# Moving the DRAM casts of the weights: one per four slots in steps 3 to 12, none in steps 13 to 16, the rest from the second chunk's second step on

## The chip, the cores and the metric

The kernel runs on the 8 cores of one Trainium2 chip. Each core has a matrix engine (TensorE, PE), a vector engine (VectorE, DVE), a scalar engine (ScalarE, ACT), a general engine (GpSimd, POOL) and a sequencer that only issues transfers (SyncE, SP). Sixteen DMA engines per core move the data for all of them. Every core computes two of the sixteen sequences and no core talks to another. The metric is the device time of the slowest core, in microseconds.

## The reference, cut

A state-space layer (Mamba) with a post-norm, then a feed-forward layer with a low-rank term and a second post-norm, on x of shape 16 x 2048 x 1024:

```
xc, z = split(x @ W_in.T)                     # 2 x 2048 columns
xc    = silu(conv4(xc) + conv_b)
xp    = xc @ W_x.T                            # B (16), C (16), dt (1)
delta = softplus(dt * w_dt + b_dt)
h_t   = exp(delta*A) * h_(t-1) + (delta*xc) B_t      # 16 states per channel
y     = (sum_n h_t C_t + D*xc) * silu(z)
x     = layernorm(x + y @ W_out.T)
h     = gelu(x @ W1.T + scale * (x @ m1.T) + b1)
x     = layernorm(x + h @ W2.T + scale * (h @ m2.T) + b2)
```

`m1` and `m2` are built from 16 tokens of the sequence (the low-rank term).

## The kernel before

**Tiling.** A core's 2 x 2048 tokens are cut into 8 chunks of 512 tokens (`NC = 8`, four chunks to a sequence, `CPS = 4`). The 2048 inner channels are 16 tiles of 128. One tile of one chunk is a *step*; steps are numbered through, 0 to 127, and chunk c has the steps 16c to 16c + 15. A step has 8 *slots* (`NP`), so a chunk has 128 slots (`CS`). In each slot DVE runs two recurrences (`tensor_tensor_scan`, L1014: one state of 128 channels over 512 tokens), in every second slot one product of four states with C (`hm`, L1024), and in the fifth slot of a step the gate of the step before (`yy`, L1035). PE feeds the recurrences (`ps_dbx`, L528) and sums the states (`ps_y`, L548), ACT makes the decays (`da`, L859).

**What shares the slots.** While chunk c runs its recurrences, the other matrix work is laid into the same slots by `plan()`: the input projection and convolution of chunk c + 1 (`X1`, `X2`, `Z`), and all that follows the recurrences of chunk c - 1 (`OUT`, `F1`, `F2` and the statistics `ST`). So chunk 0 (slots 0 to 127) carries no `OUT`, `F1` or `F2`, and chunk 1 (slots 128 to 255) is the first that does. Every engine goes through the slots in order; what an engine has to do in a slot stands in `pe_at`, `act_at`, `pool_at`. POOL is held to DVE's pace: in each even slot s it waits until the product s/2 is made.

**Where weights come from.** The weights lie in DRAM as float32 (`wts`, 122 tiles of 128 x 1024). The projections that run before slot 128 take theirs from a transfer issued by POOL that converts on the way (`WFIRST`, `wr<-wts`, L1076, 49 tiles). Every later use takes a bfloat16 copy, `w_scr`, in DRAM. This copy is made once, by *casts*: DRAM-to-DRAM transfers issued by POOL (`w_cast`, L1081, `w_scr<-wts`), 31 of them, each of four tiles (1 MB written) but one of two. The input gets a bfloat16 copy too, one cast per chunk (`XCAST`, `x_cast`, L1062, `xt_scr<-xt`, 1 MB).

**Who reads the copies.** SP goes through all later tiles in one fixed order and loads each into a ring of 8 buffers (`wr`, `NW = 8`; L492 for a weight tile, L479 for the small diagonals, L485 for the residual from `xt_scr`). It waits for the buffer to be given free by PE and, at the first tile of a group, for the group's cast. The ring is its only lead: it can be at most 8 tiles ahead of PE. SP also loads the input of chunk 2 and later into `xT` (L457, eight transfers); for chunk 2 these stand ahead of all weight tiles in its queue, and wait for `XCAST` 2 and for the last projection that reads the old `xT` (Z of step 15, which stands in slot 114). Between them PE uses 13 tiles in step 16, 19 in step 17, 16, 12, 14, 16 and 14 in steps 18 to 23, and about 14 in each later step; in steps 13, 14 and 15 it uses one each.

**Where the casts stand.** `place_casts` sets the slot in which POOL issues each. Before the change cast k of `groups` stands in slot 24 + 5k: slots 24, 29, ... 174. The groups come in the order of their first use, with the last two quarters of `T_X` and `T_Z`, the second half of `T_CD` and all of `T_W2` at the end.

Of the kernel before, what the change touches and what calls it, by code (L numbers as in the profile page):

```python
# [26 lines left out]
NP = 8  # L27
G = NC * NDT
CS = NDT * NP
# [5 lines left out]
T_X, T_Z, T_WO, T_W1, T_W2, T_CD, T_DD, N_TILES = 0, 16, 32, 48, 80, 112, 120, 122  # L35
# [145 lines left out]
def place_casts(pe, pool):  # L181


    order = [(s, tile) for s in sorted(pe) for it in pe[s] for tile, _ in tiles_of(it)]
    n_direct = next(i for i, (s, tile) in enumerate(order) if s >= CS)
    first = -CS - 1
    pool[first].append(("XFIRST", 0))
    for k in range(n_direct):
        pool[first if k < NW else max(order[k - NW][0], -CS) + 1].append(("WFIRST", k))
    pool[-40].append(("XFIRST", 1))  # L190
    groups = [T_WO, T_WO + 4, T_X, T_Z, T_CD, T_DD, T_WO + 8, T_WO + 12, T_X + 4, T_Z + 4]
    groups += [T_W1 + 4 * k for k in range(8)] + [T_X + 8, T_Z + 8, T_X + 12, T_Z + 12, T_CD + 4]
    groups += [T_W2 + 4 * k for k in range(8)]
    pool[2 * NP + 4].append(("XCAST", 0))
    pool[10 * NP + 4].append(("XCAST", 1))
    for k, tile in enumerate(groups):
        pool[3 * NP + 5 * k].append(("CAST", tile, 2 if tile == T_DD else 4))
    for c in range(2, NC):
        pool[(c - 2) * CS + 13 * NP + 6].append(("XCAST", c))
    return n_direct  # L200


# [42 lines left out]
def tiles_of(it):  # L245

    if it[0] == "X1":
        return [(T_X + it[2], True)]
    if it[0] == "Z":
        return [(T_Z + it[1] % NDT, True)]  # L250
    if it[0] == "X2" and it[1] >= 2:
        return [(("CD", it[2]), True)]
    if it[0] == "DD":
        return [(("DD", it[1] % NDT), False)]
    if it[0] == "OUT":
        q = 2 * it[3] + it[4]
        mine = [(T_WO + 2 * q, False), (T_WO + 2 * q + 1, False)]
        return mine + ([(("RES",) + it[1:4], True)] if it[4] == 1 else [])
    if it[0] == "F1":
        return [(T_W1 + 2 * it[3], False), (T_W1 + 2 * it[3] + 1, False)]  # L260
    if it[0] == "F2":
        return [(T_W2 + (2 * it[3]) * 4 + it[4], False), (T_W2 + (2 * it[3] + 1) * 4 + it[4], False)]
    return []
# [19 lines left out]
def build_nc():  # L283
# [13 lines left out]

    pe_at, act_at, pool_at = plan()
    n_direct = place_casts(pe_at, pool_at)
    bank_of = banks(pe_at, act_at)  # L300
    w_order, w_gone, w_at = stream(pe_at, bank_of)
# [1030 lines left out]
```

## Time and profile before

| | |
|---|---|
| Times of three runs | 3660.56, 3676.93, 3946.54 us |
| Median | 3676.93 us |
| Profiled execution, its own time | 3667.33 us |
| Span of its slowest core (core 6) | 3665.8 us |
| Spans of the eight cores | 3642.7 to 3665.8 us |
| Mean granted TensorE clock | 0.953 to 0.957 |
| PE, DVE, ACT, POOL busy on core 6 | 85%, 84%, 77%, 26% |

One plain remark on the three times: the third came from an execution in which a die ran at a lower clock, which happens with any kernel; the other two and the profiled one are undisturbed.

The span is what lies between the first and the last instruction of a core. The end of each gate (`yy`, L1035) marks a step, so the distance of two gates is the time of a step, and two chunks that run the same program can be laid beside each other. An engine's row in a list gives start and length; what stands in brackets is how long it sat idle before and what ended that. In the rows of transfers, "to landing" is the time from issue until the data is there.

### The profile page before, as it was taken

The page shows a single profiled execution, that of the slowest core. Times are in us where ns is not written, and L with a number is a line of the kernel's source. Part 1 is how long each engine was busy: PE and PEld are TensorE (multiplying, and loading weights), DVE is VectorE, ACT ScalarE, POOL GpSimd, SP SyncE. Part 2 cuts the span into 40 slices and gives each one's busy share as a digit, 9 for nine tenths or more (in the row PEclk, how much of TensorE's full clock was granted, in tenths as well). Part 3 has the DMA queues.
Part 4 walks back from the last instruction along what each step waited for, and adds up shares of the span by engine and source line. Part 5 has one row for each costly group of instructions (what it writes and reads, how often), then busy time and mean ns, then how long its engine had stood idle before and what let it go on. Part 6 is the DMA issues. An engine that isn't in the chain of part 4 may idle for free.

```text
span 3665.8 us, 72241 instructions; the slowest of 8 cores (3642.7 to 3665.8 us)
## 1 busy us (share of the span) xinstructions
PE 3125.9 (85%) x21688; PEld 2065.9 (56%) x21688; DVE 3074.1 (84%) x2688; ACT 2816.3 (77%) x4264; POOL 940.2 (26%) x1331
## 2 busy tenths in 40 slices
PE   6666578988989889989889889899889888788897
PEld 2333245656656556666566556666556565565676
DVE  0999978889989899999989899898999899898600
ACT  4777667887888968888888978978788877878332
POOL 6222313022421133120431234211430224101132
PEclk9888789999999999999999999999999999998998
DMA  7468788546545465446545465455544444443576
GB/s 117 70 95 104 119 168 169 144 140 157 157 125 143 131 159 150 135 130 170 151 134 145 128 165 148 119 148 147 165 139 143 138 133 137 117 123 111 158 226 181
DMA packets 300965, 517.04 MB, mean 141 GB/s; under 512 B 45784, under 2 KB 97368, under 8 KB 299104
## 3 DMA queue, kind: packets, MB, share of 16 engines
q1 hardware_dynamic: 268544, 421.07, 40.3%
q0 software_dynamic: 13984, 72.32, 12.8%
q10 hardware_dynamic: 18064, 19.02, 1.9%
q8 instruction: 191, 3.13, 0.4%
q14 instruction: 182, 1.49, 0.1%
HBM read 550.90 MB, written 57.29 MB: 166 GB/s over the span
## 4 chain that ended last, share of the span: by engine, by line
PE 42%; DVE 19%; ACT 19%; issue 16%; DMA 2%; POOL 1%; DVEq 1%; ACTq 1%; SPq 0%; POOLq 0%
DVE hq L1014 13%; PE ps_f L710 7%; PE ps_f L674 7%; ACT da L859 7%; PE ps_dbx L528 6%; PE ps_f L560 6%; PE ps_y L548 5%; DVE hm L1024 5%; ACT L859 3%; ACT hh L919 2%; PE ps_f L616 2%; ACT L919 1%; DMA wr<-w_scr 1%; PE ps_f L575 1%; ACT L792 1%
## 5 line engine op out<-in xcount | busy, mean ns | idle before, releaser
L1014 DVE TENSOR_TENSOR_SCAN hq<-da,state,ps_dbx 128x512 bf16<-128x512 f16 x1536 | 1855.1, 1262 | 244.4 <-PE ps_dbx L528 209.4
L859 ACT ACTIVATE da<-delta,prm_sb 128x512 f16<-128x512 f32 x2048 | 1349.7, 713 | 135.8 <-DVE hq L1014 124.4
L528 PE MATMUL ps_dbx<-dp,vt 128*128 128x256 bf16 x4096 | 639.3, 281 | 261.8 <-DVE hq L1014 257.0
L1014 DVE TENSOR_TENSOR_SCAN hq<-da,ps_dbx 128x512 bf16<-128x512 f16 x512 | 585.0, 1197 | 131.6 <-PE ps_dbx L528 130.9
L528 PEld LDWEIGHTS ps_dbx<-dp,vt 128*128 128x128 bf16 x4096 | 378.0, 100 | 493.4 <-issue 403.0
L1024 DVE TENSOR_TENSOR hm<-hq,crep 128x2048 bf16<-128x2048 bf16 x512 | 641.5, 1253 | 0.2 <-DVE hq L1014 0.2
L548 PE MATMUL ps_y<-hm,cst_sb 128*128 128x512 bf16 x2048 | 562.4, 400 | 2.9 <-DVE hm L1024 2.9
L674 PE MATMUL ps_f<-y,wr 128*128 128x256 bf16 x4096 | 500.3, 277 | 67.8 <-ACT hh L919 25.6
L1147 POOL CAST state<-hq 128x4 f32<-128x4 bf16 x384 | 71.7, 187 | 1805.6 <-DVE hm L1024 1805.6
L560 PE MATMUL ps_f<-xT,wr 128*128 128x512 bf16 x2048 | 498.7, 388 | 42.0 <-DMA wr<-wts 16.5
L674 PEld LDWEIGHTS ps_f<-y,wr 128*128 128x128 bf16 x4096 | 398.6, 99 | 171.3 <-issue 97.8
L710 PE MATMUL ps_f<-hh,wr 128*128 128x256 bf16 x4096 | 485.2, 273 | 1.8 <-DMA wr<-w_scr 1.2
L710 PEld LDWEIGHTS ps_f<-hh,wr 128*128 128x128 bf16 x4096 | 398.9, 98 | 79.5 <-issue 3.0
L560 PEld LDWEIGHTS ps_f<-xT,wr 128*128 128x128 bf16 x2048 | 200.6, 99 | 275.9 <-issue 73.9
L859 ACT ACT_TABLE_LOAD x256 | 328.4, 1283 | 7.0 <-DVE hq L1014 2.5
L873 ACT COPY rr<-ps_f 128x512 f32<-128x512 f32 x128 | 74.5, 582 | 305.8 <-PE ps_f L724 183.8
L548 PEld LDWEIGHTS ps_y<-hm,cst_sb 128*128 128x128 bf16 x2048 | 210.6, 103 | 174.0 <-issue 39.7
L616 PE MATMUL ps_f<-yy,wr 128*128 128x256 bf16 x2048 | 252.0, 277 | 21.0 <-DMA wr<-w_scr 9.6
L616 PEld LDWEIGHTS ps_f<-yy,wr 128*128 128x128 bf16 x2048 | 202.8, 100 | 67.2 <-issue 26.8
L919 ACT ACTIVATE hh<-ps_f,prm_sb 128x256 bf16<-128x256 f32 x512 | 200.5, 474 | 40.2 <-PE ps_f L686 38.8
L1121 POOL TENSOR_TENSOR vv<-delta,xc 128x512 bf16<-128x512 f32 x128 | 147.7, 1154 | 243.4 <-DVE hm L1024 211.8
L919 ACT ACT_TABLE_LOAD x115 | 147.5, 1283 | 76.4 <-PE ps_f L686 75.1
(92 smaller groups left out, 2549.5 us busy)
## 6 DMA issues: line engine op xcount, KB each, us to landing
wr<-w_scr SPq DMA_DIRECT2D x1487, 256.0 KB, 3.0
w_scr<-wts POOLq DMA_DIRECT2D x30, 1024.0 KB, 12.8
crep<-c_scr POOLq DMA_DIRECT2D x32, 512.0 KB, 4.1
outT<-rr ACTq DMA_DIRECT2D x16, 1024.0 KB, 5.7
wr<-wts POOLq DMA_DIRECT2D x49, 256.0 KB, 5.4
wr<-w_scr SPq DMA_DIRECT2D x96, 128.0 KB, 2.5
xt_scr<-xt POOLq DMA_DIRECT2D x8, 1024.0 KB, 12.8
wr<-xt_scr SPq DMA_DIRECT2D x64, 128.0 KB, 3.3
```

The costliest lines, as they stand in the source:

```text
L528: i = t.matmul(ps_dbx[s % 2][:, tb * 256:(tb + 1) * 256], vt[g % 2][:, tb * P:(tb + 1) * P], dp[:, k * 1024 + tb * 256:k * 1024 + (tb + 1) ...
L548: i = t.matmul(ps_y[:], ident, hm[:, at:at + T], start=False, stop=(q == 3 and n == 3))
L560: i = t.matmul(ps[:], w[:, k * P:(k + 1) * P], xT[c % 2][:, k * T:(k + 1) * T], start=(k == 0), stop=(k == NKD - 1))
L616: i = t.matmul(ps[:, k * TH:(k + 1) * TH], w[:, kt * P:(kt + 1) * P], y_tile(c * NDT + e * 8 + kt)[:, h * TH:(h + 1) * TH], start=(k == 0 ...
L674: i = t.matmul(ps[:, e * TH:(e + 1) * TH], w[:, k * P:(k + 1) * P], half(y1, h, k), start=(e == 0 and k == 0), stop=False)
L710: i = t.matmul(ps[:, e * TH:(e + 1) * TH], w[:, kt * P:(kt + 1) * P], hh[:, (k * 8 + kt) * TH:(k * 8 + kt + 1) * TH], start=(k == 0 and e ...
L859: s_.activation(da[:, (e % NDA) * T:(e % NDA + 1) * T], delta[g % 2][:], AF.Exp, scale=a_col(dt, 2 * k + n)).then_inc(s_da, 1)
L873: s_.copy(rr[h][:, at], ps[:]).then_inc(s_resid, 1)
L919: i = s_.activation(hh[:, m * TH:(m + 1) * TH], ps[:, e * TH:(e + 1) * TH], AF.Gelu, bias=prm[:, C_B1 + m:C_B1 + m + 1])
L1014: v.tensor_tensor_scan(hq[:, at:at + T], da[:, (e % NDA) * T:(e % NDA + 1) * T], ps_dbx[s % 2][:, n:2 * T:2], first, OP.mult, OP.add).then ...
L1024: v.tensor_tensor(hm[:, (qi % NHM) * 4 * T:(qi % NHM + 1) * 4 * T], hq[:, (qi % 2) * 4 * T:(qi % 2 + 1) * 4 * T], crep[:, q * 4 * T:(q + 1 ...
L1121: p.tensor_tensor(vv[:], delta[g % 2][:], xc_tile(g), OP.mult).then_inc(s_v, 1)
```

## The change

In `place_casts` the slots of the casts are given by a list in place of 24 + 5k:

```diff
     pool[2 * NP + 4].append(("XCAST", 0))
-    pool[10 * NP + 4].append(("XCAST", 1))
-    for k, tile in enumerate(groups):
-        pool[3 * NP + 5 * k].append(("CAST", tile, 2 if tile == T_DD else 4))
+    pool[24 * NP + 6].append(("XCAST", 1))
+
+    at = list(range(3 * NP, 13 * NP, 4)) + list(range(17 * NP + 2, 24 * NP, 4))
+    for s, tile in zip(at, groups):
+        pool[s].append(("CAST", tile, 2 if tile == T_DD else 4))
     for c in range(2, NC):
-        pool[(c - 2) * CS + 13 * NP + 6].append(("XCAST", c))
+        pool[(c - 2) * CS + (12 if c == 2 else 13) * NP + 6].append(("XCAST", c))
```

Written out, with the order of the groups unchanged:

| | before | after |
|---|---|---|
| Casts 0 to 19 | slots 24 to 119, every 5th | slots 24 to 100, every 4th |
| Casts 20 to 30 | slots 124 to 174, every 5th | slots 138 to 178, every 4th |
| XCAST 1 | slot 84 | slot 198 |
| XCAST 2 | slot 110 | slot 102 |
| Casts in slots 103 to 137 | 104, 109, 110 (XCAST), 114, 119, 124, 129, 134 | none |

The other engines' programs are the same. Lines behind the edit have numbers larger by 2 in the changed kernel.

On POOL, at the end of chunk 0 (slots 124 to 129), before the change. `dp` and `crep` are the diagonals and the C rows made for the next chunk, `state` keeps the end of a chunk, `w_scr<-wts` is a cast:

```order
L1130 TENSOR_TENSOR dp<-cst_sb,bt 128x1024
L1139 DMA crep<-c_scr 128x2048
L1147 CAST state<-hq 128x4
L1130 TENSOR_TENSOR dp<-cst_sb,bt 128x1024
L1081 DMA w_scr<-wts 32x16384
L1130 TENSOR_TENSOR dp<-cst_sb,bt 128x1024
L1139 DMA crep<-c_scr 128x2048
L1147 CAST state<-hq 128x4
L1130 TENSOR_TENSOR dp<-cst_sb,bt 128x1024 x2
L1139 DMA crep<-c_scr 128x2048
```

The same place after:

```order
L1132 TENSOR_TENSOR dp<-cst_sb,bt 128x1024
L1141 DMA crep<-c_scr 128x2048
L1149 CAST state<-hq 128x4
L1132 TENSOR_TENSOR dp<-cst_sb,bt 128x1024 x2
L1141 DMA crep<-c_scr 128x2048
L1149 CAST state<-hq 128x4
L1132 TENSOR_TENSOR dp<-cst_sb,bt 128x1024 x2
L1141 DMA crep<-c_scr 128x2048
```

Only the cast is gone from between them. On POOL again, in steps 19 and 20 (the casts of slots 154 and 159), before the change (`var` and `rr` belong to the statistics, `vv` is a product for the recurrences, `e2z` and `su` to the low-rank term):

```order
L1081 DMA w_scr<-wts 32x16384
L1147 CAST state<-hq 128x4
L1210 TENSOR_TENSOR e2z<-e2v,prm_sb 16x1024
L1202 TENSOR_TENSOR su<-rows,msk 16x1024
L1090 COPY halo<-xpre 128x3
L1094 COPY xpre<-halo 128x3
L1147 CAST state<-hq 128x4
L1121 TENSOR_TENSOR vv<-delta,xc 128x512
L1147 CAST state<-hq 128x4
L1081 DMA w_scr<-wts 32x16384
```

And after (slots 154, 158 and 162):

```order
L1083 DMA w_scr<-wts 32x16384
L1149 CAST state<-hq 128x4
L1212 TENSOR_TENSOR e2z<-e2v,prm_sb 16x1024
L1204 TENSOR_TENSOR su<-rows,msk 16x1024
L1092 COPY halo<-xpre 128x3
L1096 COPY xpre<-halo 128x3
L1149 CAST state<-hq 128x4
L1083 DMA w_scr<-wts 32x16384
L1123 TENSOR_TENSOR vv<-delta,xc 128x512
L1149 CAST state<-hq 128x4 x2
L1083 DMA w_scr<-wts 32x16384
```

The first cast stands in slot 154 in both. The next stands a slot earlier than before (158 for 159), ahead of `vv`, and the one of slot 162 follows in two more rows.

## Rows read from the trace of the kernel before

**Rows 1.** Cores: span, mean granted TensorE clock

```profile
core 6: 3665.8 us, clock 0.953
```

**Rows 2.** Timeline of DVE, gates: start us, length us, line; chunks 1 and 5

```profile
444.73 0.68 DVE L1035 TENSOR_TENSOR yy<-ps_y,zs 128x512 bf16<-128x512 f32 x1
...
471.95 0.68 DVE L1035 TENSOR_TENSOR yy<-ps_y,zs 128x512 bf16<-128x512 f32 x1
...
513.25 0.69 DVE L1035 TENSOR_TENSOR yy<-ps_y,zs 128x512 bf16<-128x512 f32 x1
...
690.84 0.68 DVE L1035 TENSOR_TENSOR yy<-ps_y,zs 128x512 bf16<-128x512 f32 x1
...
929.91 0.68 DVE L1035 TENSOR_TENSOR yy<-ps_y,zs 128x512 bf16<-128x512 f32 x1
...
2173.47 0.69 DVE L1035 TENSOR_TENSOR yy<-ps_y,zs 128x512 bf16<-128x512 f32 x1
...
2197.64 0.68 DVE L1035 TENSOR_TENSOR yy<-ps_y,zs 128x512 bf16<-128x512 f32 x1
...
2226.71 0.68 DVE L1035 TENSOR_TENSOR yy<-ps_y,zs 128x512 bf16<-128x512 f32 x1
...
2383.27 0.69 DVE L1035 TENSOR_TENSOR yy<-ps_y,zs 128x512 bf16<-128x512 f32 x1
...
2617.42 0.69 DVE L1035 TENSOR_TENSOR yy<-ps_y,zs 128x512 bf16<-128x512 f32 x1
```

**Rows 3.** Chain that ended last, pieces: start us, length us, what

```profile
474.38 19.63 DMA wr<-w_scr
...
518.82 9.09 DMA wr<-w_scr
...
544.04 14.84 DMA wr<-w_scr
```

**Rows 4.** Waits of DVE, 445 to 513 us: total us, times, longest us

```profile
DVE hq L1014 <- PE ps_dbx L528: 18.6, 6, 6.6
```

**Rows 5.** Timeline of SP around the start of chunk 1

```profile
415.99 17.66 SPq L457 DMA_DIRECT2D xT<-xt_scr  x8
...
480.64 6.95 SPq L485 DMA_DIRECT2D wr<-xt_scr  x1
487.69 5.55 SPq L479 DMA_DIRECT2D wr<-w_scr  x1
```

**Rows 6.** Transfers issued, 445 to 513 us: median us to landing

```profile
wr<-w_scr SPq DMA_DIRECT2D x18, 256.0 KB, 8.5
w_scr<-wts POOLq DMA_DIRECT2D x4, 1024.0 KB, 13.5
```

**Rows 7.** Transfers issued, 2170 to 2227 us (start of chunk 5)

```profile
wr<-w_scr SPq DMA_DIRECT2D x16, 256.0 KB, 2.8
```

**Rows 8.** Windows: stretch, us, busy us per engine, PEclk, DMA share, GB/s

```profile
445.00:472.00 27.00, 21.28 (x96) 10.43 (x96) 23.45 (x22) 20.30 (x32) 14.17 (x17) 0.74 1.08 218
513.00:691.00 178.00, 149.77 (x1029) 99.19 (x1027) 149.27 (x128) 144.94 (x222) 46.09 (x77) 0.94 0.74 162
2227.00:2383.00 156.00, 141.03 (x1008) 93.75 (x1007) 145.34 (x126) 141.21 (x215) 51.89 (x74) 0.99 0.47 136
```

**Rows 9.** Timeline of POOL: casts of slots 134 and 174

```profile
507.56 0.54 POOL L1081 DMA_DIRECT2D w_scr<-wts  x1
...
638.77 0.54 POOL L1081 DMA_DIRECT2D w_scr<-wts  x1 [0.25 <-issue]
```

**Rows 10.** Windows in chunk 0, columns as in rows 8

```profile
200.00:300.00 100.00, 66.05 (x332) 32.58 (x332) 100.00 (x92) 79.08 (x115) 28.78 (x63) 0.88 0.64 90
```

**Rows 11.** Timeline of DVE in chunk 0: gates of steps 1 and 12

```profile
141.89 0.68 DVE L1035 TENSOR_TENSOR yy<-ps_y,zs 128x512 bf16<-128x512 f32 x1
...
394.52 0.68 DVE L1035 TENSOR_TENSOR yy<-ps_y,zs 128x512 bf16<-128x512 f32 x1
```

**Rows 12.** Tile wts, 325 to 328 us (slot 84): the cast behind XCAST 1

```profile
DMA to landing us min/median/max: 23.3/23.3/23.3
```

## The prediction

> **What bounds the kernel now.** I read the spans first, then the gates step by step, then the waits and the chain of waits where the steps are long, and last the transfers under them. Core 6 is the slowest at 3665.8 us [rows 1]; the profiled execution took 3667.33 us, 1.5 us more, and 9.6 us less than the median of the runs shown. My sum is made against 3667.3. Undisturbed executions of this kernel lie between 3660.6 and 3676.9, so about 8 us of scatter either way belong to any forecast.
>
> In chunk 0 DVE is the bound: 100.00 busy of 100 us [rows 10], and eleven steps take 394.52 - 141.89 = 252.6 us, 23.0 each [rows 11]. The casts there cost nothing. In chunk 1 this is no longer so. The cleanest measure is chunk 5, which runs the same program as chunk 1 (it is the second chunk of its sequence, and carries the low-rank work of a first one) but has no weight cast in it. From gate to gate, chunk 1 takes 929.91 - 471.95 = 458.0 us and chunk 5 takes 2617.42 - 2197.64 = 419.8 us [rows 2]. With the interval ahead of each (27.2 against 24.2) the excess is 41.2 us. It falls into three parts [rows 2]:
>
> 1. The boundary, two intervals: 513.25 - 444.73 = 68.5 us, against 2226.71 - 2173.47 = 53.2. Excess **15.3**.
> 2. The next six steps: 690.84 - 513.25 = 177.6, against 2383.27 - 2226.71 = 156.6. Excess **21.0**.
> 3. The nine behind them, without casts: 239.1 against 234.2. Excess 4.9, from how statistics and activations fall against each other; I leave it alone.
>
> The chain of waits says what the first two are. Between 474 and 559 us it runs three times through a weight load, for 19.6, 9.1 and 14.8 us [rows 3], and DVE waits 18.6 us for PE's products between 445 and 513 [rows 4]: PE goes through its slots in order and stands at a weight tile, and the products for DVE are queued behind it. The loads are late because SP's transfers crawl beside the casts: a 256 KB tile lands 8.5 us after its issue there [rows 6] and 2.8 us at the same place of chunk 5 [rows 7], and single issues of SP last 5.6 and 7.0 us [rows 5]. The eight `xT` loads at the head of SP's queue take 17.7 us, until 433.7 [rows 5], so the ring gets its first tile of chunk 1 only then, close to the moment from which 13 and then 19 tiles a step are wanted.
>
> **The change, part by part.**
>
> *Slots 103 to 137 get no cast.* The last cast and XCAST 2 now stand in slots 100 and 102, and land before slot 110. Even if XCAST 2 landed earlier, `xT` could be loaded only when Z of step 15 (slot 114) is done, so SP starts at about 416 as before; but its eight loads and the first eight tiles then run alone, and every tile of steps 16 and 17 lands in about 3 us. That is what chunk 5 has, so the 15.3 us should go, save one thing: PE comes out of the light chunk 0 at a granted clock of 0.74 [rows 8], an average between its two levels of 1.2 and 2.4 GHz, where chunk 5 starts warm. Bounds: nothing to 15.3. I take **-14**.
>
> *Casts 20 to 30 now run one per four slots from slot 138 to 178.* Part 2 held nine casts, those of slots 134 (issued at 507.6, its transfer after 513) to 174 [rows 9]. Excess per cast: 21.0 / 9 = 2.3 us. After, it holds eleven: 11 x 2.3 = 25.7, that is +4.7 by count alone. They are also closer. A cast lands 13.5 us after issue [rows 6] and four slots of a 26 to 28 us step are 13 to 14 us, so there is practically always one in flight, and SP gets no stretch to refill the ring; five slots left it 3 to 4 us. I add 1.3 for that, a choice: **+6**. Bounds of the price of one cast: nothing (the ring starts full now, and between 513 and 691 the idle time of DVE is mostly shared with activations), and 15.3 / 4 = 3.8 us, the price at the boundary, where four casts [rows 6] met a ring that was behind. That gives -21 to +21 for this part.
>
> *XCAST 1 goes from slot 84, where it was free, to slot 198*, in a step that wants 14 tiles. The price of a cast is 0 to 2.3 there; I take **+1**.
>
> *Chunk 0 has 20 weight casts in slots 24 to 100 where it had 16, and one input cast fewer there.* What waits behind them on POOL's queue are the 49 direct weight loads. Is the queue able to? Two casts issued together in slot 84 were both done 23.3 us after the second one's issue [rows 12], so one takes at most some 11.7 us, and four slots of a 23.0 us step are 11.5, with some 0.7 MB of direct loads per step on top. That looks full, but a cast behind one in service needs less than its full time to landing (23.3 - 13.5 = 9.8 us), the share of the DMA engines was 0.64 [rows 10], and the direct loads have the ring's 8 tiles, about three steps (69 us), of lead. POOL itself spends 0.54 us on an issue [rows 9]. Cost **0**; if the lead were used up, PE would stand for `wr<-wts` in steps 9 to 12 and DVE with it; a backlog of 3 us a step would need more than ten steps to eat it.
>
> *Casts come late for their readers?* The tightest is the last quarter of `T_W2`: cast in slot 178, its ring buffer free in slot 199, 21 slots (some 70 us) for a transfer of 13.5. Nothing waits there. SP's and POOL's instructions are otherwise the same.
>
> Sum: -14 + 6 + 1 = -7, so 3667.3 - 7 = **3660 us**.
>
> **Row and rule.** In 513 to 691 us the DMA engines were busy 0.74 x 178 = 132 us, in chunk 5's six steps 0.47 x 156 = 73 us [rows 8]: the nine casts took 59 us of them, 6.5 us each. The Trainium skill ("DMA: Bandwidth & Descriptors", section "Issuing engines are not separate DMA queues") says that transfers of all issuing engines end on the same 16 DMA engines and interleave. It speaks against this change in so far as moving a cast moves its work and removes none. A step after would then hold 73/6 + 2 x 6.5 = 25.2 us of transfers in the 26.1 us that it takes without casts. If busy engines were all that counts, casts would be hidden and part 2's 21.0 us would vanish too. The measured 2.3 us per cast at a share of 0.74 says that the landing time, not the sum, is what is paid; I follow the row.
>
> **The rivals.**
>
> *R1, the casts become nearly free (the excess of part 2 is the echo of the late start).* The chain's weight waits at 519 and 544 us [rows 3] come while SP is still catching up from the boundary. If a ring that starts full stays full, casts at a share of 25.2/26.1 cost perhaps 0 to 1 us each: 11 x 0.9 = 10, so -14 - 21 + 10 + 1 = -24, and 3643 us. For it: no excess is needed by the engines' busy time. Against: tiles land slowly as long as a cast is in flight, and the ring's lead of 8 tiles is half a step.
>
> *R2, slower: casts without a gap starve the ring in steps 17 to 22.* The price of a cast rises from 2.3 to the boundary's 3.8 us, since one is always in flight while 12 to 19 tiles a step are wanted: 11 x 3.8 - 21 = +21, so -14 + 21 + 1 = +8, and 3675 us. It decides from (14 + 21 - 1) / 11 = 3.1 us per cast on.
>
> *R3, the boundary is not the casts' doing.* The cold clock and POOL's `dp` and `crep` work (14.2 us busy in 27 [rows 8]) hold it up: the first part brings only -3, and -3 + 6 + 1 = +4, 3671 us. Against it stand the 19.6 us through a weight load in the chain.
>
> **How the numbers follow.** My forecast 0.47 (own range 3652 to 3668), R1 0.28, R2 0.15, R3 0.10. The 8-in-10 range reaches from R1's 3643 to between R2's 3675 and what the scatter adds: 3642 to 3680. All cases lie within 2% (73 us), which is about what a measurement of this kernel can tell from no change; the whole excess of 41 us is less than that. So within 2% has 0.98, faster and slower 0.01 each.
>
> **What would show it.** The two intervals at the boundary should be near 24 to 26 and 29 us where they were 27.2 and 41.3, with no wait of PE for `wr<-w_scr` ahead of slot 138, tiles landing in about 3 us there and the `xT` loads taking well under 17.7 us. The six steps behind should take about 182 us; 167 would be R1, 198 R2. Chunk 0 should stay at 23.0 us a step. I would be wrong if direct loads stall chunk 0, or if the weight waits simply reappear at slot 138 with the length that they had at slot 130.

## The result and the profile after

The changed kernel is slower: 1.0045 times the time of the kernel before, with a 95% interval of 1.0024 to 1.0066, which is 9 to 24 us on 3660. I had forecast 3660 us, a gain of 7. Its profiled execution took 3671.8 us (before 3667.3); the shortest of 22 runs of each took 3668.3 us, and 3657.5 us in the kernel before. Runs in which a die ran at a lower clock are left out of every ratio and range of times here; they are so many that plain medians say nothing.

The gates of core 7, the slowest of the profiled execution, are these (timeline of DVE: start us, length us; gates of steps 1, 12, 14, 16, 17, 22 and 31):

```profile
142.66 0.68 DVE L1037 TENSOR_TENSOR yy<-ps_y,zs 128x512 bf16<-128x512 f32 x1
...
402.13 0.68 DVE L1037 TENSOR_TENSOR yy<-ps_y,zs 128x512 bf16<-128x512 f32 x1
...
450.51 0.68 DVE L1037 TENSOR_TENSOR yy<-ps_y,zs 128x512 bf16<-128x512 f32 x1
...
504.51 0.68 DVE L1037 TENSOR_TENSOR yy<-ps_y,zs 128x512 bf16<-128x512 f32 x1
...
542.07 0.68 DVE L1037 TENSOR_TENSOR yy<-ps_y,zs 128x512 bf16<-128x512 f32 x1
...
699.53 0.68 DVE L1037 TENSOR_TENSOR yy<-ps_y,zs 128x512 bf16<-128x512 f32 x1
...
943.37 0.68 DVE L1037 TENSOR_TENSOR yy<-ps_y,zs 128x512 bf16<-128x512 f32 x1
```

One core is not enough, since the cores of one execution differ by up to 17 us in chunk 1 (gates 15 to 31: 446.4 to 463.9 us before, 453.3 to 467.2 after). Read in the same way on all eight cores of each profiled execution, the mean lengths of the stretches between these gates are:

| us, mean of 8 cores | before | after | difference |
|---|---|---|---|
| start to gate 1 | 141.3 | 141.6 | +0.3 |
| gates 1 to 12 (chunk 0) | 253.2 | 260.6 | **+7.4** |
| gates 12 to 14 | 49.2 | 48.4 | -0.8 |
| gates 14 to 16 (boundary) | 65.8 | 54.0 | **-11.8** |
| gates 16 to 22 (tail of the casts) | 176.4 | 189.6 | **+13.2** |
| gates 22 to 31 | 239.6 | 241.1 | +1.5 |
| gate 31 | 925.4 | 935.3 | +9.9 |

The boundary went as forecast. SP's eight loads of `xT` take 3.6 us in place of 17.7 [rows 5], and 256 KB tiles land in 3.3 us in place of 8.5 [rows 6]:

```profile
421.32 3.64 SPq L459 DMA_DIRECT2D xT<-xt_scr  x8
425.11 0.32 SPq L494 DMA_DIRECT2D wr<-w_scr  x1
```

```profile
wr<-w_scr SPq DMA_DIRECT2D x15, 256.0 KB, 3.3
```

(The second fence is from the transfers issued from 445 to 502 us.) But the stall is back 35 us later, in step 17, beside the casts of slots 138 and 142: gates 16 to 17 take 35.7 us (mean of 8 cores), where they take 23.9 in the kernel without casts there (number 5). The waits of PE and of DVE from 502 to 545 us on core 7 (total us, times, longest us):

```profile
PE ps_f L618 <- DMA wr<-w_scr: 6.8, 1, 6.8
PE ps_y L544 <- DMA wr<-w_scr: 3.7, 1, 3.7
```

```profile
DVE hq L1016 <- PE ps_dbx L530: 14.1, 5, 7.9
DVE hq L1016 <- ACT da L861: 1.2, 1, 1.2
```

And chunk 0, which I had called free, is not. There PE waits for POOL (core 7, 140 to 400 us) in each of the steps 3 to 12, nine times some 0.4 us and once 0.7. DVE waits for PE's products for 6.3 us, where core 6 of the kernel before has 0.4:

```profile
PE ps_f L577 <- POOL xpre L1096: 4.4, 10, 0.7
```

```profile
DVE hq L1016 <- PE ps_dbx L530: 6.3, 10, 0.8
```

In the kernel before, the same stretch (core 6) has two such waits of PE for POOL:

```profile
PE ps_f L575 <- POOL xpre L1094: 0.8, 2, 0.4
```

The timeline of POOL shows what PE waits for. In the first slot of each of the steps 3 to 12 the changed kernel has a cast (every fourth slot from 24 on). Its issue is the last work of that slot, and so it stands between the convolution's diagonal (L1105) and the copy of the halo columns into `xpre` (L1096), the first work of the next slot, which PE's convolution needs:

```profile
225.00 1.04 POOL L1105 TENSOR_TENSOR cdiag<-cst_sb,prm_sb 128x512 bf16<-128x512 bf16 x1
225.99 0.55 POOL L1083 DMA_DIRECT2D w_scr<-wts  x1
226.54 0.20 POOL L1092 COPY halo<-xpre 128x3 bf16<-128x3 bf16 x1
226.66 0.19 POOL L1096 COPY xpre<-halo 128x3 bf16<-128x3 bf16 x1
```

With the old distance of five slots a cast fell into that place once in eight casts.

### The profile page after: what moved, and what is told of

It reads as the page before. It is cut to its first block, busy times and chain, and to the rows that moved or that the text cites. A ratio compares the mean times of both kernels' runs of the same rounds, so it can differ in the third digit from the quotient of the medians.

```text
span 3670.1 us, 72241 instructions; the slowest of 8 cores (3653.1 to 3670.1 us)
## 1 busy us (share of the span) xinstructions
PE 3130.5 (85%) x21688; PEld 2067.1 (56%) x21688; DVE 3074.8 (84%) x2688; ACT 2819.5 (77%) x4264; POOL 940.9 (26%) x1331
## 4 chain that ended last, share of the span: by engine, by line
PE 42%; DVE 19%; ACT 18%; issue 15%; DMA 3%; POOL 1%; DVEq 1%; ACTq 0%; SPq 0%; POOLq 0%
DVE hq L1016 12%; PE ps_f L676 7%; PE ps_f L712 7%; ACT da L861 7%; PE ps_dbx L530 6%; PE ps_f L562 6%; PE ps_y L550 6%; DVE hm L1026 5%; ACT L861 3%; ACT hh L921 2%; DMA wr<-w_scr 2%; PE ps_f L577 2%; PE ps_f L618 2%; PE ps_f L633 1%; DVE yy L1037 1%
## 5 line engine op out<-in xcount | busy, mean ns | idle before, releaser
L676 PE MATMUL ps_f<-y,wr 128*128 128x256 bf16 x4096 | 500.2, 277 | 70.5 <-ACT hh L921 25.7
## 6 DMA issues: line engine op xcount, KB each, us to landing
w_scr<-wts POOLq DMA_DIRECT2D x30, 1024.0 KB, 13.2
```

Source lines behind the costliest of these rows:

```text
L676: i = t.matmul(ps[:, e * TH:(e + 1) * TH], w[:, k * P:(k + 1) * P], half(y1, h, k), start=(e == 0 and k == 0), stop=False)
```

## Experiments

Each table entry is the mean of the eight cores of one profiled execution; "end" is gate 31. Each ratio is to runs of the kernel before taken beside it; only those of the changed kernel, number 8 and number 12 differ from 1 by more than their interval.

| us | 1 to 12 | 14 to 16 | 16 to 22 | 22 to 31 | end | ratio to before, 95% |
|---|---|---|---|---|---|---|
| before | 253.2 | 65.8 | 176.4 | 239.6 | 925.4 | |
| after | 260.6 | 54.0 | 189.6 | 241.1 | 935.3 | 1.0045 [1.0024, 1.0066] |
| 1: chunk 0 one slot later | 252.6 | 53.2 | 184.4 | 240.5 | 921.2 | 0.9986 [0.9952, 1.0020] |
| 2: tail every 5 slots | 260.2 | 53.8 | 180.1 | 239.6 | 923.6 | 1.0002 [0.9968, 1.0035] |
| 3: tail slots of before | 259.9 | 61.5 | 171.6 | 239.8 | 921.6 | 1.0041 [0.9995, 1.0087] |
| 4: three tail casts | 260.4 | 54.0 | 180.8 | 240.3 | 924.8 | |
| 5: no tail cast | 260.4 | 54.0 | 168.5 | 240.6 | 912.3 | |
| 6: tail from slot 150 | 252.6 | 53.1 | 181.2 | 245.5 | 922.5 | 0.9998 [0.9983, 1.0014] |
| 7: 25 early, 6 late | 252.5 | 53.8 | 172.0 | 239.2 | 907.5 | 0.9992 [0.9958, 1.0027] |
| 8: 28 early, 3 late | 252.5 | 53.2 | 171.7 | 239.1 | 906.6 | 0.9954 [0.9936, 0.9973] |
| 9: one cast, slot 138 | 260.0 | 53.8 | 171.7 | 240.1 | 914.9 | |
| 10: one cast, slot 154 | 260.4 | 53.9 | 167.6 | 241.0 | 912.4 | |
| 11: two, 138 and 142 | 260.1 | 54.0 | 181.7 | 240.0 | 925.5 | |
| 12: as 8, with a gap | 252.5 | 54.3 | 155.3 | 232.1 | 884.9 | 0.9877 [0.9818, 0.9935] |

For number 7 the table has cores 4 to 7 only: in its profiled execution cores 0 to 3 had a granted clock of 0.93.

**1. Chunk 0's casts one slot later.**

```diff
-    at = list(range(3 * NP, 13 * NP, 4)) + list(range(17 * NP + 2, 24 * NP, 4))
+    at = list(range(3 * NP + 1, 13 * NP, 4)) + list(range(17 * NP + 2, 24 * NP, 4))
```

> The changed kernel with the 20 weight casts of chunk 0 one slot later (25, 29, ... 101 in place of 24, 28, ... 100); everything else as in the changed kernel. In its trace chunk 0 grew: gate of step 1 to gate of step 12 takes 260.6 us (mean of eight cores) where it took 253.2. Theory P (place): a cast's issue (0.55 us of POOL) stands in the first slot of each step just between the conv diagonal and the copy of the halo columns, PE waits 0.41 us for the halo, and DVE is left short. One slot later the halo stands ahead of the cast, so the eleven steps return to 253 to 254.5 us with the density unchanged. Theory D (density): casts every 4 slots fill POOL's queue and the DMA engines (direct weight loads land in 11.2 us where 7.8), and the eleven steps stay at 259 to 262 us. The time of the whole falls by 7 us by P and by nothing by D.

252.6 us, from 252.1 to 252.8 on the eight cores: theory P, and nothing of D. The number of casts, their distance and their load are the same, and they take as long to land: medians of 140 to 400 us are 8.8 to 14.9 us on the eight cores, 8.8 to 14.2 in the changed kernel. On core 0:

```profile
w_scr<-wts POOLq DMA_DIRECT2D x19, 1024.0 KB, 14.9
```

The direct weight loads, which theory D names, do land sooner (5.6 to 7.9 us, where the changed kernel has 6.1 to 12.5), but PE waits for none of them in either kernel. On POOL the halo copies now stand right behind the diagonal, with the cast behind both, and PE's waits name no halo any more:

```profile
223.47 1.04 POOL L1105 TENSOR_TENSOR cdiag<-cst_sb,prm_sb 128x512 bf16<-128x512 bf16 x1
224.46 0.18 POOL L1092 COPY halo<-xpre 128x3 bf16<-128x3 bf16 x1
224.58 0.18 POOL L1096 COPY xpre<-halo 128x3 bf16<-128x3 bf16 x1
224.71 0.59 POOL L1078 DMA_DIRECT2D wr<-wts  x1
225.30 0.51 POOL L1083 DMA_DIRECT2D w_scr<-wts  x1
```

The gates 16 to 22 also fell by 5.2 us, which neither theory said, since nothing was changed there. I did not follow this up. So a difference of about 5 us in that column does not by itself speak for the tail's casts.

**2. The tail every five slots.**

```diff
-... + list(range(17 * NP + 2, 24 * NP, 4))
+... + list(range(17 * NP + 2, 24 * NP, 5))
```

> The changed kernel with its last eleven weight casts one per five slots (138, 143, ... 188) in place of one per four (138 to 178). Their number and their first slot stay. In the changed kernel gate 16 to gate 22 takes 189.6 us (mean of eight cores), 33.0 more than the 156.6 of the same steps of chunk 5, or 3.0 per cast; in the kernel before 176.4, that is 19.8 for nine casts, 2.2 each. Theory D (density): a gap between casts lets SP refill the ring, the price falls back to 2.2 each: the excess over gates 16 to 23 falls by 6 to 10 us, so 180 to 184 for gate 16 to 22 and no more than 1 to 2 us more behind it. Theory N (number): each cast costs 3.0 wherever it stands in these steps; nine casts lie ahead of gate 22 then, so gate 16 to 22 falls to about 184 but gate 22 to 31 grows from 241 to 247, and the end of chunk 1 stays within 2 us of 935 us. The end of chunk 1 tells them apart: 925 to 929 by D, 933 to 937 by N.

180.1 us, as theory D has it, and an end at 923.6, below its range and far from that of N (gate 22 stands in slot 188, so ten or all eleven casts lie ahead of it and not nine; the end is what tells the two apart): the same eleven casts from the same first slot cost 11.7 us less in all. A fixed price per cast is refuted. Whether the larger distance did it or the other slots that ten of the casts now have, this run does not tell apart; number 3 has casts five slots apart too, in slots 134, 139 and 144, and its gates 16 to 17 take 25.5 us where they take 33.0 here.

**3. The tail in the slots of before.**

```diff
-... + list(range(17 * NP + 2, 24 * NP, 4))
+... + list(range(124, 175, 5))
```

> The changed kernel with its last eleven weight casts in the slots they had before the change (124, 129, ... 174), so three casts stand at the boundary again; chunk 0 stays dense and XCAST 1 at slot 198. If the three parts of the change add up as separate terms: gates 1 to 12 at 260.6 us, the boundary (gates 14 to 16) back from 54.0 to about 66, gates 16 to 22 back from 189.6 to about 176, and the end of chunk 1 at 935 us plus or minus 3: the quiet boundary and the dense tail cancel. If the excess behind the boundary were an echo of the late start and not the casts' own price, the changed kernel should have had less of it, not more; this run has the late start again and would be above 190 there.

The boundary is back at 61.5 and the tail at 171.6, so the two trade with each other as said, but both came out 4 to 5 us below the expectation, and the end at 921.6 where I had 935 +- 3: a miss. The terms do not simply add: three casts at the boundary cost 7.5 us here (61.5 against 54.0), and the tail's slots are those of the kernel before, which has 176.4. That the stretch behind a bad boundary is shorter than behind a good one is against an echo of the late start.

**4 and 5. Fewer and no casts in the tail.** The list of casts is cut and the loads are sent to another copy of the same size, so these kernels leave out the conversion of some weights and compute other values with the same instructions; only the lengths of their stretches are read. Number 5 also sends the loads of the last `T_X`, `T_Z` and `T_CD` groups elsewhere, which is not shown:

```diff
-    for s, tile in zip(at, groups):
+    for s, tile in zip(at, groups[:23]):        # number 5: groups[:20]
...
+                tile = tile - 32 if T_W2 <= tile < T_CD else tile
```

> The changed kernel without the eight casts of the second feed-forward weight (slots 150 to 178); the loads of that weight read the copy of the first one in its place, so this part of the computation is changed and the number and size of loads is not. Three casts are left in the tail (138, 142, 146). By a price of 3.0 us per cast, gate 16 to 22 falls from 189.6 by 24 us to about 166; if there is a fixed cost of starting (the first casts meet the two steps with 19 and 16 tiles and are dearer than the later ones) it stays above 170; if casts cost mainly by their density it ends at 158 to 163, near chunk 5's 156.6.

180.8 us, where a price of 3.0 each gave 166. Eight casts less gained 8.8 us, and the three left kept a stretch that is 24 us over chunk 5's. In its last four steps no cast was in flight. That put the reference itself in doubt.

> The changed kernel without any of its last eleven weight casts; the loads that would read them take another tile's copy of the same size, so the values of this part are changed and the number and size of the loads is not. It gives the length of gate 16 to 22 of chunk 1 without casts, for which chunk 5 (156.6 us) stood in my prediction. Theory C5 (chunk 5 is a fair reference): 156 to 159 us. Theory S (shifted): the list of work laid into chunk 1 has one item less at its front than that of chunk 5 (no second statistics of an earlier chunk), so all of it stands one slot earlier against the projections, and steps 19 to 22 are longer by themselves; the run with three casts left had 116 us in its last four steps, with no cast in flight, against 107.7 in chunk 5: 166 to 170 us. By S the price of all eleven casts is (189.6 - 168) / 11 = 2.0 us each and not 3.0, and the first three carry most of it.

168.5 us: theory S. Without a single weight cast, these six steps need 11.9 us more than chunk 5's 156.6 [rows 2]. Measured against its own base, the tail costs 176.4 - 168.5 = 7.9 us before and 189.6 - 168.5 = 21.1 after, each good to the 5 us of number 1.

**6. The tail behind the heavy steps.**

```diff
-    at = list(range(3 * NP, 13 * NP, 4)) + list(range(17 * NP + 2, 24 * NP, 4))
+    at = list(range(3 * NP + 1, 13 * NP, 4)) + list(range(18 * NP + 6, 24 * NP, 4))
```

> The changed kernel with the casts of chunk 0 one slot later, as in the first experiment (25, 29, ... 101), and with its last eleven casts from slot 150 to 190 in place of 138 to 178: same number, same distance, all behind the steps 17 and 18a that want 19 and 16 tiles. If the price lies in the heavy steps (three casts alone brought 37 us in the step of gate 17 where it takes 24 to 26), gate 16 to 22 falls from the 184.4 us of the first experiment to 172 to 177 and the end of chunk 1 from 921.2 to 911 to 916. If each cast costs the same wherever it stands in chunk 1, the end of chunk 1 stays at 919 to 923.

A miss: the end is at 922.5 and not at 911 to 916; it lies where a price that is the same everywhere puts it (919 to 923). Step 17 is clean (23.9 us), but the eleven casts cost 181.2 + 245.5 - 168.5 - 240.6 = 17.6 us in later steps. SP's waits there name only PE and no cast, so the casts were in time; the chain between 560 and 740 us on core 1 runs through two weight loads again:

```profile
564.20 19.36 DMA wr<-w_scr
...
684.13 15.66 DMA wr<-w_scr
```

So it is not the 19 tiles of step 17 alone: a row of casts four slots apart cost 17.6 us here and 21.1 from slot 138.

**9, 10 and 11. One and two casts by themselves**, on the kernel of number 5:

```diff
-... + list(range(17 * NP + 2, 24 * NP, 4))
+... + [138]            # number 10: [154], number 11: [138, 142]; groups cut to match
```

> The kernel without tail casts (gate 16 to 22 there: 168.5 us, on seven cores of eight within 0.1 of 168.8) with one cast put back, in slot 138, where step 17 with its 19 tiles is under way. Its values are changed as there, its loads are not. If a cast's price is set by how many tiles the step wants, this one costs 4 to 8 us: 173 to 177. If the price needs casts that follow each other closely, it costs 0 to 2: 168.5 to 171.

> The same with the one cast in slot 154 (step 19, which wants 12 tiles). By the number of tiles wanted it costs 0 to 1.5 us: 168.5 to 170. Slots 138 and 154 have the same place in their steps, so POOL's order does not tell them apart; the same price in both would mean that the place in chunk 1 does not matter.

> The same with two casts, in slots 138 and 142, four slots apart as in the changed kernel. Three casts (138, 142, 146) brought gate 16 to 22 from 168.5 to 180.8 us. If one cast is hidden and the second finds the ring drained, two cost 8 us or more where one costs under 2; if prices add, two cost twice what slot 138 alone costs.

One cast in slot 138 costs 3.2 us, which lies between my two cases (4 to 8, and 0 to 2), one in slot 154 nothing (-0.9), and the two of slots 138 and 142 together 13.2 us. On core 3, around step 17, the waits of PE for a tile are, with one cast (500 to 532 us)

```profile
PE ps_y L546 <- DMA wr<-w_scr: 3.1, 1, 3.1
```

and with two (503 to 543 us)

```profile
PE ps_f L564 <- DMA wr<-w_scr: 5.6, 1, 5.6
PE ps_y L546 <- DMA wr<-w_scr: 3.0, 1, 3.0
```

DVE is idle 5.5 and 13.3 us for PE's products in them:

```profile
DVE hq L1018 <- PE ps_dbx L532: 5.5, 3, 2.4
```

```profile
DVE hq L1018 <- PE ps_dbx L532: 13.3, 5, 6.5
```

One might say that the first cast uses up the ring's lead and the second finds none. SP's queue on core 3 says otherwise. The first cast lands at 511.1 us; SP then issues seven loads in a row, and from 513.2 us on it waits again for PE to give a buffer free, so every free buffer had its load under way when the second cast was issued at 513.1. What stalls PE is the next load, issued at 515.25 us, which lands after 15.1 us (the chain of waits of 500 to 545 us):

```profile
515.25 15.10 DMA wr<-w_scr
```

The same load with one cast lands in 5.2 us. So a load that meets a cast can take longer than the ring's eight tiles last in a step that wants 19 (an estimate: 8 of 19 tiles in 23.9 us are 10 us), and whether slot 142 needs slot 138 before it for that is open: no run has a cast in 142 alone. What is shown is that the price is not one per cast, and that nearly two thirds of what the eleven of the changed kernel cost (21.1 us) are there with its first pair alone; the other nine add 7.9 us.

**7, 8 and 12. Versions made from this.**

```diff
 (number 8)
-    at = list(range(3 * NP, 13 * NP, 4)) + list(range(17 * NP + 2, 24 * NP, 4))
+    at = list(range(5, 14 * NP + 2, 4)) + list(range(20 * NP, 24 * NP, 8))
-    pool[24 * NP + 6].append(("XCAST", 1))
+    pool[1].append(("XCAST", 1))
 (number 7, XCAST 1 in slot 1 as well)
+    at = list(range(5, 13 * NP, 4)) + list(range(19 * NP, 24 * NP, 6))
 (number 12, in post_items, on number 8)
     if c > 0:
         its += [("ST", c - 1, 1, 2)]
+    else:
+        its += [("GAP",)]
```

> A version made from what the runs have shown so far: the casts start in slot 5 and not in 24, one per four slots and never in a step's first slot (5, 9, ... 101: 25 casts), none until slot 151, and only six behind (152, 158, ... 182); XCAST 1 in slot 1. If chunk 0 hides any cast that keeps clear of a step's first slot, gates 1 to 12 stay at 252 to 254 us, the boundary at 53 to 54, and gate 16 to 22 falls to 168 to 172: the end of chunk 1 at 905 to 910, 15 to 20 us before that of the kernel before, so 3640 to 3648 us beside a before of 3656 to 3661. If the early casts hold up the direct weight loads of the first steps, gate 1 comes 5 us or more later and the gain is halved.

> As the last one, but the casts of chunk 0 go on to slot 113 (28 casts) and only three are left behind (160, 168, 176). It tells how long the quiet before the boundary has to be: if transfers of chunk 2's input (from slot 114 on) and the first eight tiles still run alone, the boundary stays at 53 to 55 us and the tail loses 2 to 4 us more; if the casts of slots 105 to 113 delay them, the boundary grows by 2 to 6 us.

Chunk 0 takes 25 and 28 casts, four slots apart and clear of each step's first slot, at 252.5 us, and gate 1 is not later (140.7 us in number 8). In number 8 the boundary stays at 53.2, so a cast as late as slot 113 does it no harm, and the end of chunk 1 comes 18.8 us before that of the kernel before; the whole is faster by 0.27 to 0.64%, 10 to 23 us. That the tail loses 2 to 4 us more than in number 7 was a miss: it has 171.7 us with three casts and 172.0 with six, some 3 us over the kernel without any. Number 7 ends chunk 1 at 907.5 us on cores 4 to 7, but its times ran from 3638.9 to 3681.0 us, and its ratio cannot be told from 1.

> The version with 28 casts in chunk 0 (gate 16 to 22: 171.7 us, 17 us less than the kernel before in all) with one empty place put into the list of work of chunk 0's later stages, where every other chunk has its second statistics, so that chunk 1's work stands in the same slots as chunk 5's. By theory S (the shift makes chunk 1 slower than chunk 5 without any cast) gate 16 to 22 falls by 8 to 12 us to 160 to 164, and the time of the whole with it to 3630 to 3637 beside 3656 to 3661 of before. If the difference between the chunks has another cause it stays at 171 to 173.

155.3 us, below the range that I gave, as the time of the whole is, and 232.1 behind it where all other versions have 239 to 245. Theory S stands: beside number 8, which differs in nothing else, one empty place at the front of chunk 1's list gives back 16.4 + 7.0 = 23.4 us in these two stretches and 21.7 at the end of chunk 1, as much as the eleven casts of the changed kernel cost. The three casts of slots 160 to 176 are still there, and the six steps are no longer than chunk 5's without a cast (156.1 us, mean of eight cores). So the prices of casts found above hold for the shifted list; what the rows of casts cost with the empty place in was not run. The slowest core of the profiled execution:

```profile
core 3: 3619.3 us, clock 0.959
```

Its times are 3618.3 to 3624.4 us beside 3653.0 to 3692.0 of the kernel before, a ratio of 0.9877 [0.9818, 0.9935].

## Why the prediction was wrong

- **The boundary: right.** Forecast -14, measured -11.8. The first interval at the boundary (25.7 us), the second (28.3 us) and the `xT` loads (3.6 us) are as said. Part of the excess there was not paid on all cores alike: core 6, on which I sized it, had 68.5 us where the mean of the eight was 65.8.
- **Chunk 0 at nothing: the step that failed.** I looked at POOL's queue and the DMA engines, where the worry was not needed (number 1), and took POOL's 0.54 us per issue as free because POOL is 26% busy. What stands *behind* the issue on POOL is the halo copy, and PE's convolution waits for it, 0.41 us at a time. Where the matmuls behind that wait ran at the lower clock, PE's next product came too late for DVE; where they ran at full clock it did not (last section). Measured +7.4. The order of instructions on POOL, which was to be had beforehand, shows the cast between `cdiag` and `halo` in each of the steps 3 to 12 of the changed kernel. My text named the direct loads as the way in which chunk 0 could stall; it was another.
- **Price of a cast in the tail: both its factors were off, and the shape.** "It runs the same program as chunk 1" was wrong by one item of a list: 11.9 of the 21.0 us that I divided by nine casts were no cast's doing (number 5), and number 12 shows that they were the missing place's. The price before was 7.9 / 9 = 0.9 us and not 2.3. Then I multiplied, 11 x 2.3 + 1.3, forecast +6, and measured +13.2: 21.1 us for eleven casts, 11.8 of it in step 17, where the pair of slots 138 and 142 stands (numbers 5 and 11). A price per cast, whatever its size, was the wrong shape; whether the pair's distance or its place makes it dear is not shown. I had seen that "SP gets no stretch to refill the ring", and put 1.3 us on it as a choice.
- **XCAST 1: about right.** Forecast +1; gates 22 to 31 are 1.5 us longer. Leaving out 6 and 12, the kernels with it in slot 198 have 239.6 to 241.1 us there and the two with it in slot 1 (7 and 8) 239.1 and 239.2, so its price is not told from their scatter.
- **The third part, left alone, was the shift too.** I put 4.9 us of chunk 1's excess over chunk 5 down to how statistics and activations fall against each other. With the empty place these nine steps take 232.1 us (number 12) where all others have 239 to 245, so it was part of the same misalignment.
- **The sum.** By the measured terms 0.3 + 7.4 - 0.8 - 11.8 + 13.2 + 1.5 = +9.8 us at the end of chunk 1, which is inside the 9 to 24 us of the ratio. The profiled execution itself came out only 4.5 us longer than that of before; from gate 31 to the end the cores of one execution differ by 8 to 10 us.
- **The rivals.** R1 (casts nearly free) is gone: the tail got longer. The row was to be followed and not the count of busy DMA time. R2 is nearest, in sign and in that the denser casts cost more, but its +8 comes close to the measured +9.8 by luck: it had +21 for the tail, which is +13.2, and nothing for chunk 0, which was in no rival. R3 (the boundary is not the casts' doing) is refuted by the 54.0 us. I put 0.15 on R2, because the price that it needed, 3.1 us by the wrong base, looked far from 2.3.

## What to carry to other kernels

An instruction that only issues a transfer can cost what stands behind it on its engine: before it is put into a schedule with a period, look at which place of the period it falls into, since a stride of 4 in a step of 8 slots hits the same place each time and a stride of 5 spreads it. Background transfers next to a ring of loads are not priced one by one: here one cost 3.2 us or nothing and a pair 13.2, and six or three of them, spread out, some 3. So put them where the ring idles (here, before the first chunk's end) and measure what is left with none of them. And before a stretch serves as the reference for another, compare their lists of work item by item, or measure the stretch with the suspect taken out.

## What the runs showed that I had not expected

- 28 DRAM-to-DRAM casts, all but one of 1 MB written, four slots (11.5 us) apart, cost nothing that can be seen in a chunk whose weights come by the same queue: 252.5 us for eleven steps (before: 253.2). And this though a queue builds up: the casts of number 8 land 26.8 us after issue and the direct weight loads 19.1 us (medians of 100 to 440 us on core 7), and PE waits for none of these loads.

```profile
w_scr<-wts POOLq DMA_DIRECT2D x26, 1024.0 KB, 26.8
wr<-wts POOLq DMA_DIRECT2D x23, 256.0 KB, 19.1
```

- The same 0.41 us of delay costs DVE nothing or up to 1.5 us, and the granted clock decides. I followed PE's waits for the halo between 140 and 400 us on all eight cores, 80 in the changed kernel and 16 in the one before. Behind 35 of the 96 the twelve matmuls that follow (four of the convolution, eight of the projection) took 2.75 us, and DVE waited for nothing; behind 61 they took 4.2 to 4.4 us, and DVE waited 0.4 to 1.5 us each time. In the changed kernel those are 54 waits and 6.7 us a core, in the kernel before 7 waits and 0.5, and the difference is most of the 7.4 us of chunk 0. Two of them on core 7, the matmuls and DVE's wait behind the first:

```profile
250.58 1.69 PE L577 MATMUL ps_f<-xpre,cdiag 128*128 128x512 bf16 x4 [0.41 <-POOL xpre L1096]
252.06 2.95 PE L562 MATMUL ps_f<-xT,wr 128*128 128x512 bf16 x8
...
275.16 1.03 PE L577 MATMUL ps_f<-xpre,cdiag 128*128 128x512 bf16 x4 [0.41 <-POOL xpre L1096]
276.03 1.89 PE L562 MATMUL ps_f<-xT,wr 128*128 128x512 bf16 x8
```

```profile
255.63 2.33 DVE L1016 TENSOR_TENSOR_SCAN hq<-da,ps_dbx 128x512 bf16<-128x512 f16 x2 [0.62 <-PE ps_dbx L530]
```

  The mean granted clock was 1.00 ahead of both; behind the first it fell to 0.61, behind the second it stayed (the column behind POOL's):

```profile
245.00:250.50 5.50, 3.27 (x19) 1.42 (x16) 5.50 (x6) 4.04 (x7) 2.08 (x6) 1.00 0.56 82
250.60:255.00 4.40, 4.40 (x14) 1.72 (x15) 4.40 (x4) 2.09 (x3) 1.30 (x4) 0.61 1.12 119
270.00:275.00 5.00, 2.86 (x17) 1.23 (x14) 5.00 (x5) 5.00 (x10) 1.99 (x6) 1.00 0.56 108
275.20:277.90 2.70, 2.70 (x14) 1.26 (x15) 2.70 (x3) 2.05 (x3) 0.29 (x1) 1.00 1.83 194
```

  Without a wait for the halo (the kernel before, numbers 1 and 8) the same twelve matmuls took 2.75 us in 219 of 224 cases. So the wait and the fall of the clock go together; why it fell behind 61 of the waits and not behind the other 35 is not shown. The mean clock of 200 to 400 us does not tell it: 0.83 to 0.85 on the cores of the changed kernel, 0.84 to 0.86 before.

- One slot's shift of the background work against the projections is worth 22 us of 3660 at the end of chunk 1, with the same instructions (numbers 8 and 12).
